# One tile of four of the experts' combination scaled on ScalarE and added on GpSimd, in both mixtures of a four-layer kernel

## The reference, cut to what matters

```python
# second layer, its mixture
_, idx = jax.lax.top_k(logits + lb_bias, K)                  # K = 2 experts of 8
w = sigmoid(logits at idx); w = w / (sum(w) + 1e-06)
moe_out = jnp.einsum('ned,ne->nd', expert_out, we)           # two experts' rows, weighted, summed
return moe_out + shared
...
x = x + jnp.tanh(g_ffn[1]) * _L1_ffn_ref(_layernorm(x, axis=-1), ...)
x = x + jnp.tanh(g_xattn[2]) * _L2_xattn_ref(_layernorm(x, axis=-1), ...)   # reads x right behind the first mixture
...
x = x + jnp.tanh(g_ffn[3]) * _L3_ffn_ref(_layernorm(x, axis=-1), ...)       # the second mixture, the last step of all
return x
```

## Time and profile before

| | |
|---|---|
| median of 3 runs | 952.01 us (951.39 to 959.11) |
| the profiled execution, its own time | 955.21 us |
| its span from first to last instruction | 953.5 us |
| TensorE busy | 782.0 us, 82% |
| VectorE busy | 630.0 us, 66% |
| ScalarE busy | 335.5 us, 35% |
| GpSimd busy | 283.1 us, 30% |
| chain that ended last | TensorE 51%, VectorE 24%, ScalarE 8% |

### The profile page before, as it was taken

How to read it: one execution, slowest core, us unless ns; L and a number is a source line. 1 busy time by engine, 2 the same in 40 slices (tenths; PEclk the granted TensorE clock), 3 DMA queues, 4 the chain that set the end, 5 groups by cost and what they waited for, 6 DMA issues and landing times.

```text
span 953.5 us, 13463 instructions
## 1 busy us (share of the span) xinstructions
PE 782.0 (82%) x4216; PEld 587.8 (62%) x4216; DVE 630.0 (66%) x1698; ACT 335.5 (35%) x622; POOL 283.1 (30%) x284
## 2 busy tenths in 40 slices
PE   7787998975888777579992899978999988779992
PEld 6555666653356656379972777645666665479971
DVE  3578889866997666365637746548657555666646
ACT  2322221225653662135540553313233221225530
POOL 1038113160001556614561101226000333304550
PEclk9899999997999999789995999989999999989995
DMA  9619950000001002247426000051000111214427
GB/s 281 121 61 374 345 185 0 1 1 1 0 1 34 1 0 82 97 117 251 135 79 220 1 1 1 1 162 49 1 1 1 44 46 45 89 51 142 133 85 257
DMA packets 55474, 83.30 MB, mean 87 GB/s; under 512 B 14688, under 2 KB 44384, under 8 KB 55136
## 3 DMA queue, kind: packets, MB, share of 16 engines
q1 hardware_dynamic: 48496, 63.52, 21.3%
q0 software_dynamic: 6912, 18.95, 5.6%
HBM read 61.41 MB, written 37.95 MB: 104 GB/s over the span
## 4 chain that ended last, share of the span: by engine, by line
PE 51%; DVE 24%; ACT 8%; issue 7%; DVEq 6%; DMA 2%; POOL 1%; another core or an unknown queue 0%; SPq 0%; ACTq 0%; POOLq 0%
PE sh L700 14%; PE ob L700 11%; PE sh L1076 6%; PE ob L1076 6%; PE pt L668 4%; DVE sm L1796 2%; DVE work L1800 2%; DVE work L1788 2%; DVE mx L1786 2%; ACT work L1337 2%; DVEq L1785 2%; PE pt L700 2%; DVE x L2038 2%; PE pt L1068 2%; PE sh L1095 2%
## 5 line engine op out<-in xcount | busy, mean ns | idle before, releaser
L700 PE MATMUL sh<-area,xnT 128*128 128x512 f32 (+1 forms) x384 | 140.6, 517 | 7.7 <-issue 5.2
L533 POOL TENSOR_TENSOR rstd<-var,minush 128x4 f32<-128x4 f32 (+1 forms) x29 | 30.6, 1056 | 317.8 <-DVE var L1659 317.8
L700 PE MATMUL ob<-area,work 128*128 128x256 f32 x512 | 118.0, 384 | 7.6 <-ACT work L1274 7.6
L700 PEld LDWEIGHTS ob<-area,work 128*128 128x128 f32 x512 | 97.5, 192 | 34.1 <-issue 20.6
L597 POOL DMA_INDIRECT yt<-xn,work x80 | 76.9, 962 | 120.0 <-ACT xn L1518 88.6
L700 PEld LDWEIGHTS sh<-area,xnT 128*128 128x128 f32 x384 | 65.6, 204 | 61.2 <-issue 58.0
L1337 ACT ACTIVATE work<-work 128x1024 f32<-128x1024 f32 x32 | 33.8, 1058 | 174.9 <-DVE work L1788 94.9
L588 POOL DMA_INDIRECT xg<-area,dest x64 | 63.1, 986 | 70.3 <-DVE dest L2030 52.7
L668 PE MATMUL pt<-ident,work 128*128 128x128 f32 (+1 forms) x292 | 40.8, 278 | 27.1 <-DVE work L1800 11.8
L668 PEld LDWEIGHTS pt<-ident,work 128*128 128x128 f32 (+1 forms) x292 | 32.8, 139 | 35.1 <-issue 16.0
L700 PE MATMUL ob<-area 128*128 128x256 f32 (+1 forms) x152 | 40.5, 421 | 16.7 <-issue 7.1
(11 more groups left out here) (298 smaller groups left out, 1656.6 us busy)
## 6 DMA issues: line engine op xcount, KB each, us to landing
work<-xg SPq DMA_DIRECT2D x80, 129.0 KB
area<-in_L_ffn_w SPq DMA_DIRECT2D x4, 2048.0 KB, 12.7
area<-yt SPq DMA_DIRECT2D x8, 1024.0 KB, 9.1
area<-in_L_xattn_Wq SPq DMA_DIRECT2D x2, 1024.0 KB, 9.8
x<-in_x SPq DMA_DIRECT2D x1, 2048.0 KB, 15.4
area<-in_L_xattn_Wo SPq DMA_DIRECT2D x2, 1024.0 KB, 16.1
area<-in_L_xattn_Wkv SPq DMA_DIRECT2D x2, 1024.0 KB
out<-x SPq DMA_DIRECT2D x4, 512.0 KB, 2.9
```

The source lines that it names most:

```text
L533: pool.tensor_tensor(rstd[:, n], var[:, n], minush[:, n], ALU.pow).then_inc(given, 1)
L700: mm = pe.matmul(o, a, b, start=(k == 0), stop=(k == len(lhs) - 1))
```

## The change

In each block the tile j = 3 is taken out of VectorE's `combine`. ScalarE multiplies its two halves of `y` by their weights, in place, when the block has landed, and counts `y_scaled`. GpSimd adds both halves to x, once `y_scaled` of the block and the last `o_added` of the stage are there, with a drain ahead of each add, and counts `combined_last`. In stage 3 VectorE waits for `combined_last` ahead of a block's statistics, and ScalarE's reuse of the `y` area (the keys of the next attention) waits for it too; in stage 7 SP waits for it ahead of each store.

```diff
@@ sync, after moe(7)
             for b in range(NB):
                 sp.wait_ge(combined[7], b + 1)
+                sp.wait_ge(combined_last[7], b + 1)
                 sp.dma_start(out[b]...
@@ gpsimd
+            def combine_last(stage, b):
+                pool.wait_ge(y_scaled[stage], b + 1)
+                pool.wait_ge(o_added, straight[-1].fill("o", stage, 1)[0] + 1)
+                j = TB - 1
+                for w in range(2):
+                    pool.drain()
+                    ins = pool.tensor_tensor(xt(straight[b], j), xt(straight[b], j),
+                                             y_of[b][:, j * 2 * D + w * D:j * 2 * D + (w + 1) * D], ALU.add)
+                ins.then_inc(combined_last[stage], 1)
+
             give_back(3)
             pool.memset(area3[:, 0:4096], 0.0).then_inc(v_zeroed, 1)
             for b in range(NB):
+                combine_last(3, b)
                 block_rstd(4 * NB + b, b)
...
             give_back(7)
+            for b in range(NB):
+                combine_last(7, b)
@@ scalar, fold_moves
                     if u == KEYS6:
                         act.wait_ge(combined[3], NB)
+                        act.wait_ge(combined_last[3], NB)
@@ scalar, end of moe
                 shared_act(straight[-1])
+                for b in range(NB):
+                    act.wait_ge(y_in[stage][b], 16)
+                    for w in range(2):
+                        y = y_of[b][:, (TB - 1) * 2 * D + w * D:(TB - 1) * 2 * D + (w + 1) * D]
+                        a = act.activation(y, y, ACT.Identity, bias=0.0, scale=wK[:, b * TB + TB - 1, w:w + 1])
+                    a.then_inc(y_scaled[stage], 1)
                 if stage == 3:
                     norm_move(stage, straight[-1], 2)
@@ vector, combine
                 for w in range(2):
                     dve.drain()
-                    for j in range(TB):
+                    for j in range(TB - 1):
                         ins = dve.scalar_tensor_tensor(xt(b, j), y_of[...], wK[...], xt(b, j), ALU.mult, ALU.add)
                 ins.then_inc(combined[stage], 1)
+                if stage == 3:
+                    dve.wait_ge(combined_last[3], b.u + 1)
                 if stage == 3:
                     norm_stats(b)
```

More of the change, by code:

```diff
@@ L335, in layers_kernel @@
         gate_act = sem("gate_act")
+        y_scaled, combined_last = moe_sems("y_scaled"), moe_sems("combined_last")
         f_full, f_taken, v_zeroed, fold_done = map(sem, "f_full f_taken v_zeroed fold_done".split())
```

## The result

The changed kernel is slower. Its first set of six runs has a median of 968.97 us against 951.99 us before; the ratio is 1.0149, with a 95% interval of 1.0093 to 1.0204. Two later sets of the same kernel, beside experiments, gave 1.0136 [1.0084, 1.0187] and 1.0116 [1.0081, 1.0152]. The forecast was 953.0 us, with a range of 950.0 to 956.0 and a chance of 0.96 for no change beyond the noise. The measured median lies 13 us above the top of that range.

What follows compares the result with a forecast made beforehand. VectorE was taken to bound the kernel in the first mixture's start and at the end; +0.5 at the end, 0.0 for blocks 0 and 1, +0.45 at the norm, say +1.0: 952.0 + 1.0 = 953.0 us, range 950.0 to 956.0.

Steps and rivals of the forecast that it cites:

- What bounds the kernel: Claim that time saved or lost on VectorE from 505.04 to 516.41 and from 936.16 on counts in full.
- The terms for single operations: Predicted durations: 0.49 us per ScalarE multiplication, 0.73 us per GpSimd add, 1.355 us per group of three VectorE instructions.
- The two together: GpSimd's adds and VectorE's combination hold each other off at SBUF; an add costs VectorE 0.49 us.
- The rival without exclusion: The engines do not hold each other off: -3.2 us at the run's end, -4.65 in all, 947.4 us; chance 0.10.
- the rival of a full hold: Each engine holds the port for its whole recorded time; an add costs 0.81, 958.3 us (1.17, 963.6); chances 0.08 and 0.02.
- End: VectorE's last combination, second mixture: 10.8 plus 3.9 for adds less 0.3, 14.4 us against 13.95, +0.5.
- the step on block 3: First mixture: block 3's adds meet the norm at 525.68, for which TensorE waits, and delay it by about +0.45 us.
- Block 0: First mixture: adds run amid VectorE's combination and end in time; statistics start at 508.56 against 508.55, the wait costs nothing.
- The rival that a wait takes the place of the saved work: Adds of 1.08 to 1.21 us make VectorE wait 0.3 to 0.4 twice in the first mixture; +2.5, 954.5 us; chance 0.10.
- The sign of being wrong: A gap ahead of the statistics that GpSimd ends, meaning adds slower than 0.73 or ScalarE above 0.49 us each.
- the +1.0 us: The forecast's total change for the whole kernel, +0.95 rounded, added to the median of 952.0 us.

## Why the prediction was wrong

**What bounds the kernel** was read rightly. The 5 us by which the statistics came later came out in full as time, and at the end VectorE's 14.07 us set the end.

**The terms for single operations** were right: a multiplication 0.50 us (0.49), an add 0.72 (0.73), a group of three 1.35 us (10.78 / 8, 1.355 forecast).

**The two together**: the exclusion is there. An add costs VectorE 0.41 us, forecast 0.49, so somewhat more of each is hidden than the 0.12 to 0.15 us of the earlier trace rows. The rival without exclusion (947.4) falls with the end that took 14.07 and not 10.8; the rival of a full hold (0.81 an add) falls with it too.

**End**: forecast +0.5, measured +0.1, since eight adds cost 3.3 us and not 3.9 less 0.3. "GpSimd is through with its adds at about 944" was wrong by the drain: 7.8 us behind VectorE's first instruction by the forecast, 13.0 measured (965.83 - 952.84), without effect.

**Norm of block 1** (the step on block 3): it was forecast 0.45 us longer; it is 0.66 to 0.97 longer in the three profiles of the changed kernel and 0.41 without drains:

```profile
523.29 1.78 DVE L1694 TENSOR_SCALAR xn<-x,mv,rstd 128x256 f32<-128x256 f32 x4
```

**Block 0 is the step that failed.** It said that the first add streams from 506.3 on, in the middle of VectorE's combination, that "GpSimd is done by then, so the new wait costs nothing". The drain that the diff puts ahead of each add was counted at nothing, as if it stood behind finished work. It stands behind `give_back`, that is behind 72 indirect transfers, and takes 5.95 us. This was to be read before: in the earlier trace rows the row of L622, quoted for its 200 ns, has 6.5 us of idle time, 6.0 of them by "issue", in front of a few instructions that depend on nothing but a drain. That is the first drain behind the transfers of the first mixture, which lay hidden in stage 6. The change made a drain earlier and on the path the first one, and the charge moved there. The rival that a wait takes the place of the saved work was the right mechanism, but priced at an add of 1.08 to 1.21 us, and so at 0.3 to 0.4 us for each block instead of 5.97 for the first. The sign of being wrong that the forecast named, a gap ahead of the statistics that GpSimd ends, came; of the two reasons it gave for one, slower adds or slower multiplications, neither did.

With this one term in it the forecast's sum is 952.0 + 1.0 + 5.1 = 958 us, 6.1 above the kernel before. At one clock the changed kernel is 6.5 us above it by the estimate in "The clock in all runs together", but the means of all runs are 11.3 us apart. The remaining 5 go with a lower clock, for which the forecast had no term, and what lowers it stays open.

Without the drain the first mixture does what the forecast had: the six instructions take 3.40 us (3.46 forecast), and the statistics start 3.49 us behind the first of them (3.52). The time does not confirm the +1.0 us as well: the ratios are 1.0003 and twice 1.0046 in three sets, and the intervals of the latter two begin at 1.0013 and 1.0017, just above the forecast's 1.0010. The means are 2.6 us apart, and at one clock not at all.

The Trainium skill, "GPSIMD Engine Reference", section 2.1 "Instruction dispatch", tells of about 6 us with no visible instruction, at the first call of a freshly loaded kernel of the engine. The number is the same as here, 5.95; the occasion is not. The first add runs without it when no drain stands ahead of it, and behind fewer transfers the drain costs 1.3 to 4.2 us.

## What to carry to other kernels

An engine's queue can hold a debt that nothing in the timeline shows until an instruction comes that has to settle it. Before putting a drain (or a wait) on an engine, look in the trace for the first drain behind the same kind of work on that engine, and read what it took. On GpSimd behind indirect transfers, order two instructions by a semaphore, or drain early, where nobody waits. Read a short instruction's row to its end: the idle time ahead of it was the answer here, 6.0 us by "issue", and the mean duration was only what had been looked for. And moving work to an engine that holds up the busy one while it works buys little: here two instructions saved for a block (0.80 us) were eaten by two adds (0.82 us).

## What the runs showed of the hardware

- The first drain of GpSimd behind 72 indirect transfers takes 5.9 to 6.0 us, directly behind the last of them, 8 to 10 us after it and over 90 us after it; 42 cost 4.2 us, 16 cost 2.2 us, 14 cost 1.3 us. A zero fill, adds and powers in between neither pay nor clear it, and a second drain takes 41 ns.
- A GpSimd add of 128 x 256 beside VectorE's two-operand instructions costs VectorE 0.41 us of its own 0.72.
- TensorE's mean granted clock is 0.50 in the 11 us in which it waits for the first norm of stage 4; 5.0 us more of that waiting make the kernel 6.1 us slower in the mean, 10.3 us more 10.3 (each to within some 2 us).
- Executions of one program differ by 16 us with their mean granted clock (955.66 us at 0.933, 972.07 at 0.913), some 6 us of it through one stretch at 0.75 or 1.00 in the same place. A single pair of profiles put 16.7 us to a change that costs 11.3 in the mean.
